# First attention: VectorE's neighbour sums and expert choice, moved to the middle of the next group

## The reference, cut to what matters

```
q, k, v = x_n @ Wq, x_n @ Wk, x_n @ Wv        # x_n: layer-normed rows
S = q k^T * scale;  S = where(causal, S, 0)
S = conv3x3(S) over (row, key)                # a 3 x 3 kernel for each batch and head, from ctx
S = where(causal, S, -inf);  P = softmax(S)
x = x + (P @ v) @ Wp + bp
```

## Time and profile before

| | |
|---|---|
| median of 3 runs | 1910.25 us |
| runs | 1899.67, 1910.25, 1910.5 us |
| the profiled execution's own time | 1902.02 us |
| its span, first to last instruction | 1900.3 us |
| stage of the group loop, about | 140 to 583 us of the span |
| VectorE busy in the span | 1026.5 us (54%) |
| TensorE busy in the span | 1273.0 us (67%) |
| mean granted clock of TensorE | 0.754 of full |

### The profile page before, as it was taken

How to read it: one execution, slowest core, us unless ns; L and a number is a source line. 1 busy time by engine, 2 the same in 40 slices (tenths; PEclk the granted TensorE clock), 3 DMA queues, 4 the chain that set the end, 5 groups by cost and what they waited for, 6 DMA issues and landing times. The chain is left out here.

```text
span 1900.3 us, 26101 instructions
## 1 busy us (share of the span) xinstructions
PE 1273.0 (67%) x9212; PEld 771.8 (41%) x9212; DVE 1026.5 (54%) x2918; ACT 530.6 (28%) x1053; POOL 565.7 (30%) x700
## 2 busy tenths in 40 slices
PE   1458878787884896455645399378876955787720
PEld 1223334343442785345645288222335842222210
DVE  2454455454553232599999655334433325547796
ACT  0123233332341452122312133023423522323310
POOL 6041222212334002541011600331132033155674
PEclk8588798887995998555555599669967978866665
DMA  5930000000003121433532111400001210022232
GB/s 135 389 136 1 1 1 1 1 1 0 12 7 105 41 67 48 119 100 92 136 93 61 34 60 62 130 23 1 12 18 49 67 49 23 2 63 64 79 98 74
DMA packets 73254, 116.48 MB, mean 61 GB/s; under 512 B 11565, under 2 KB 52320, under 8 KB 70624
## 3 DMA queue, kind: packets, MB, share of 16 engines
q1 hardware_dynamic: 60320, 85.24, 14.9%
q0 software_dynamic: 12800, 29.51, 5.4%
HBM read 77.03 MB, written 37.68 MB: 60 GB/s over the span
## 5 line engine op out<-in xcount | busy, mean ns | idle before, releaser
L1671 DVE CUSTOM_DVE_ANT_0 arena<-ps,far 128x512 f32<-128x512 f32 (+3 forms) x256 | 118.2, 488 | 108.6 <-PE ps L1345 107.7
L2002 POOL DMA_INDIRECT wide<-in_w_ud,arena x128 | 130.0, 1015 | 77.7 <-DVE arena L2033 40.7
L2922 PE MATMUL ps<-wide,arena 78*128 78x32 bf16 x3840 | 112.1, 187 | 51.6 <-ACT wide L3035 41.8
L1260 POOL TENSOR_SCALAR_AFFINE_SELECT arena<-arena 128x260 f32<-128x260 f32 (+1 forms) x128 | 53.7, 432 | 308.9 <-ACT arena L1538 308.8
L810 POOL DMA_INDIRECT arena<-ys_d,slot_i x64 | 61.2, 956 | 246.6 <-DMA ys_d<-arena 197.4
L2922 PEld LDWEIGHTS ps<-wide,arena 78*128 78x128 bf16 x3840 | 110.3, 104 | 58.9 <-ACT wide L3035 45.2
L983 PEld LDWEIGHTS ps<-arena 128*128 128x128 f32 (+1 forms) x1012 | 123.4, 192 | 4.0
L983 PE MATMUL ps<-arena 128*128 128x128 f32 (+1 forms) x1012 | 123.6, 275 | 0.0
L1538 ACT ACTIVATE arena<-ps 128x1024 f32<-128x1024 f32 (+1 forms) x96 | 84.6, 881 | 109.9 <-PE ps L1367 109.4
L1367 PE MATMUL ps<-arena 32*128 32x128 f32 (+3 forms) x512 | 114.2, 491 | 1.1 <-DVE arena L1690 1.1
L2543 DVE TENSOR_REDUCE arena<-ps 128x6 f32<-128x462 f32 (+1 forms) x96 | 54.9, 581 | 93.6 <-PE ps L2289 69.9
(11 more groups left out here) (498 smaller groups left out, 2632.4 us busy)
## 6 DMA issues: line engine op xcount, KB each, us to landing
arena<-low_d SPq DMA_DIRECT2D x32, 780.0 KB
xs_d<-zrow SPq DMA_DIRECT2D x1, 10240.0 KB, 30.1
ys_d<-zrow SPq DMA_DIRECT2D x1, 10240.0 KB, 55.9
arena<-xs_d SPq DMA_DIRECT2D x69, 128.0 KB, 2.0
ys_d<-arena SPq DMA_DIRECT2D x69, 128.0 KB, 1.7
arena<-in_w SPq DMA_DIRECT2D x2, 1408.0 KB
wide<-in_Wfc SPq DMA_DIRECT2D x1, 2048.0 KB, 11.8
wide<-in_Wproj SPq DMA_DIRECT2D x8, 256.0 KB, 6.5
```

The lines of the kernel that those rows point to most:

```text
L1671: ins = nc.vector.tensor_tensor_reduce(junk[:, n % 2, 384 * i:384 * i + w], ps[:, n % 2, 384 * i:384 * i + w], far[:, T - w:T], 1.0, 3 * N ...
L2002: pool.indirect_dma_start(out=rows_g[t % 4][:, h, :], out_offset=None, in_=A["w_ud"], in_offset=bass.IndirectOffsetOnAxis(ap=eidi[:, t % 8 ...
L2922: mm = nc.tensor.matmul(ps[:, 2 * (i % 3) + h // 2, col:col + 4 * HD], ring[m_ % 4][:, h * NK + p_, t % 2 * P:t % 2 * P + P], table[n // 4 ...
```

## The change: what it does

Only VectorE's order within the group loop is changed. Instructions, their number and all other engines' orders stay.

- near_scores of a unit leaves the end of group G, where it stood behind outputs and join and ahead of maximum_in, and is done in group G + 1, behind mixed_keys and ahead of the second half of the maxima. In G = 1 to 11.
- R_.norms and R_.pick stay in their groups (G = 6, 10, 14; G = 9, 13) and go from behind maximum_out to ahead of the second half of the maxima.
- R_.normed goes from the end of G = 6, 10, 14 to the middle of G = 7, 11, 15.

```diff
                         if G + 2 <= last:
                             mixed_keys(G + 2)
+                        if G and near_key(G - 1)[0] < B:
+                            near_scores(*near_key(G - 1))
                         if G % 4 == 2 and G // 4 + 2 < B:
                             norms(G // 4 + 2)
+                        if G % 4 == 2 and G >= 6:
+                            R_.norms(dve, G // 4 - 1)
+                        if G % 4 == 3 and G >= 7:
+                            R_.normed(dve, G // 4 - 1)
+                        if G % 4 == 1 and G >= 9:
+                            R_.pick(dve, ch, G // 4 - 2)
                         if G + 1 <= last:
                             maxima(G + 1, 6, 12)
                             maximum_out(G + 1)
                         if G % 4 == 2 and G // 4 + 2 < B:
                             normed(G // 4 + 2)
-                        if G % 4 == 2 and G >= 6:
-                            R_.norms(dve, G // 4 - 1)
-                        if G % 4 == 1 and G >= 9:
-                            R_.pick(dve, ch, G // 4 - 2)
                         if G % 4 == 3:
                             near_shift(G // 4)
                         if G:
                             outputs(G - 1)
                         if G % 4 == 0 and G:
                             join(G // 4 - 1)
-                        if nb < B:
-                            near_scores(nb, nt)
-                        if G % 4 == 2 and G >= 6:
-                            R_.normed(dve, G // 4 - 1)
                         if G % 4 == 1 and G >= 5:
                             projected(G // 4 - 1)
```

## The result

The changed kernel took 1944.33 us (median of 4 runs, 1940.36 to 1949.55); the kernel before, now with 4 runs, 1904.97 us (1899.67 to 1910.5). The ratio is 1.0208, 95% interval [1.0161, 1.0255]: slower by 1.6 to 2.6%, outside the range forecast (1890 to 1928, 1910 as the likeliest). The profiled execution took 1940.36 us with a span of 1938.6, 38.3 over the span of before.

What follows compares the result with a forecast made beforehand. It saw a chain passing between engines, none filling the stage, with VectorE on the path at group ends and middles. Ends -33.3, middles +31.6, query clock -20.0 and falls +25 gave +3 us: 1910 us, range 1890 to 1928.

Steps and rivals of the forecast that it cites:

- The ends: Group ends G = 0 to 10: TensorE's holes shrink once near_scores leaves, -33.3 us (22.1 before query matmuls, 11.2 before transposes).
- the query matmuls: After the group ends: query matmuls slowed by low clock return to full clock, -20.0 us.
- The middles by length: Mid-group, before the ninth maximum matmul: moved steps stall TensorE by their own length, nothing covering near_scores, +31.6 us.
- The falls: Mid-group in G = 1, 3, 4, 5, 7, 8, 10, 11: six of eight new holes lower TensorE's clock, +25 us.
- Rival (c): Clock falls in all eight middles and stays low into the next query matmuls: +38 us, 1940 to 1948, chance 0.11.
- The router steps: Mid-group: R_.normed +2.2 us (G = 7, 11), R_.norms +0.7 (G = 6, 10, 14), R_.pick +1.5 (G = 13).

Runs made afterwards that it cites:

- all middles filled: Changed kernel, first shifted projection repeated 4 to 6 times in G = 0 to 10, eighth maximum matmul 6 to 20 times in G = 11 to 13: 1884.51 us.

## Why the prediction was wrong

**The ends: right.** -33.3 us were forecast from near_scores' leaving. The waits before the query matmuls went from 32.5 to 10.2 us over the stage, where -22.1 were forecast, and the row of 13.1 us before the transposes is gone. The holes before the queries are 0.4 us now, and the query matmuls went from 61.60 to 43.34 us, -18.3, where -20.0 were forecast (G = 7 kept a low clock).

**The middles by length: right.** +31.6; the hole is 2.93 us where 2.94 were forecast, 3.20 at tile 0 against 3.19. Six groups (1, 3, 4, 5, 7, 8) had no fall of their own, other than at their ends, before or with all middles filled. Together they are 17.7 us shorter with the filled new order, and the forecast's terms for them without falls come to about -15.5. Over the whole stage it is -23.0 against -21.7 forecast, but so near by luck: G = 11 and 13 fell there and are 6 and 11 us longer, while G = 6 and 9, which had fallen before, are 7 and 6 us shorter.

**The falls: wrong, and this is the step that failed.** The forecast had "I take 6 of 8" new falls at 4.2 us, +25 us. The stage grew by 38.5 us, and without new falls it was to shrink by 21.7, so the falls took about 60. Both factors were too small. The clock fell in 8 of the 8, and in G = 12 and 13 as well, which the count had left out, G = 12 because near_scores isn't there, G = 13 because only its length was counted. One fall costs 5.4 to 5.6 us where the clock is back after 13.7 us (G = 4, 5, 8), above the 5.0 that I had as the upper bound, and more where it is not: against the kernel with all middles filled, G = 1, 7 and 10 are 7.0, 7.9 and 7.2 us longer. For the eight groups with a new fall that have none in their middle in the filled kernel (1, 3, 4, 5, 7, 8, 10, 12) the sum is 49.6 us; with 5.5 each for G = 11 and 13, an estimate from the others, 61. The upper bound of the forecast, 8 x 5.0 = 40, did not hold the value, and so neither did the range.

I had read the rows on which this hung as undecided: holes of 1.68 us that were followed by a fall against one of 3.08 that wasn't, and I wrote that 2.9 us lies among those, though both that were followed by a fall were shorter. The one of 3.08 us stood at the end of a group, with dense query matmuls behind it, and was the only one of ten holes of 2 us and over at ends that was not followed by a fall. In the middle of a group the longest hole that had been survived was 1.58 us, those of 1.68 were not, and the new ones were to be 2.9 or more: among its own kind the evidence leaned one way. The price was read from the second half of G = 2, a stretch whose last 3.1 us were at full clock again.

**Rival (c)** had the mechanism and the side, 1940 to 1948, with a chance of 0.11. It was right in the first half (all eight groups), wrong in the second: the clock did not stay low through the next queries, save in G = 7. That the measured 1944.33 lies in its range is luck: more falls at a higher price made up for queries at full clock.

**The router steps** were put at 4.4 us in all (2.2 + 0.7 + 1.5). Alone they cost 22. What was missing is the same: lengths of 1.1 to 1.6 us were counted and not the hole that each makes. In the changed kernel this error showed in G = 13 alone; in G = 7, 9, 10 and 11 near_scores brings the fall without them.

**The Trainium skill,** page "TensorE: Matmul & The Clock Gate", section "HAM oscillation — how this bites in real kernels", reckons half of the slow time as the price of a fall from 2.4 to 1.2 GHz. For G = 4 that gives 13.7 / 2 = 6.9 us, an estimate, against 5.4 measured: the rule is about a quarter too high here, and what I took, 4.2, as much too low. A likely reason is that part of the slow time lies beside VectorE's work, but no run parts this. With the rule and eight falls the sum would have been -22 + 55 = +33, against +38.5 measured.

## What to carry to other kernels

Of a step that is moved, ask first where its engine idles for a reason that stays, and put it there: near_scores under the query matmuls is worth 2.6%, in the middle of the maxima it costs 2.1%, with the same instructions. A stop that TensorE feels has a second price beside its length, the half-speed stretch that may follow. In the middles here, holes of 1.6 us and over were mostly followed by one, and it cost about twice a stop of 2.9 us. To judge the risk, count the holes at the same place in the kernel, apart from those in front of other work. A run with the hole filled by repeated matmuls parts the two costs without touching VectorE's order.

## What was not expected of the hardware

- The same hole of 1.57 us in G = 12 was followed by full clock in the kernel before and by a fall in the changed one, though nothing was moved in that group. In the version with the middles filled, G = 13 fell with a hole of 0.6 us. So a hole does not decide alone, but the share rises with its length. Over all eleven traces, counting holes before a maximum matmul in the middle of G = 1 to 13 and falls in the hole or within 2.2 us behind it: of 45 holes of about 0.5 us none, of 27 from 1.53 to 1.68 us 22, of 7 from 2.2 to 2.4 us 5, of 29 from 2.7 to 5.3 us all. The changed kernel had twelve of 2.2 us and over, all followed by a fall.
- With all middles filled the clock fell in G = 11 while TensorE did matmuls of 32 rows back to back, with no hole for 12 us, since the query matmuls of that group. So work alone did not keep it up.
- In the changed kernel the clock stayed low for 13.7 to 27.3 us after a fall, in G = 4 with TensorE busy for 13.2 of the 13.7 us. In the kernel before, after falls at the ends of groups, with query matmuls behind them, it was back after 3.4 to 6.8 us seven times and after 10.2 us twice.
- Work added to TensorE made the kernel faster: 61.5 us less in the stage, for matmuls that are done over into the same place.
- What lies outside the changed stage differs by up to 12 us between executions of kernels that are the same there.
